# A two-layer gated graph convolution with a routed feed-forward block: order of work on ScalarE, GpSimd, VectorE and TensorE, and the gate product in 8 steps for 12

## The reference

```python
def layer(x, row, col, edge_type, w, gate_w, root, bias):        # w: 2 x 512 x 512, from 30 basis matrices
    x_j = x[col]
    msg = [sigmoid(x_j @ gate_w[r]) [:, None] * x_j @ w[r] for r in (0, 1)]
    agg = segment_sum(where(edge_type == 0, msg[0], msg[1]), row)
    return agg + x @ root + bias
h = relu(layer(layernorm(x), ...))
x = x + layer(h, ...)
t = layernorm(x)
shared = two experts, gelu(t @ w1 + b1) @ w2 + b2, each 512 -> 64 -> 512
probs = softmax(t @ gate_w.T + gate_b)            # 8 experts
routed = sum over the two largest probs of prob * expert(t)
x = x + shared + routed
```

## Time and profile before

| | |
|---|---|
| median of 3 runs (lowest to highest) | 1832.68 us (1831.2 to 1836.52) |
| the profiled execution, its time and its span | 1830.14 us, 1828.4 us |
| TensorE matmul busy | 1614.8 us (88%) |
| VectorE busy | 911.4 us (50%) |
| ScalarE busy | 724.4 us (40%) |
| GpSimd busy | 545.7 us (30%) |
| DMA | 270.45 MB, mean 148 GB/s |

### The profile page before, as it was taken

The page is one execution under the profiler, slowest core; times in us unless marked ns, Lnnn a source line. Parts: engine busy times, 40 slices in busy tenths (PEclk is TensorE's granted clock), DMA queues, the critical chain, the costliest instruction groups (busy, mean ns, idle before and its releaser), DMA issues. The chain is left out here.

```text
span 1828.4 us, 24688 instructions
## 1 busy us (share of the span) xinstructions
PE 1614.8 (88%) x7982; PEld 1271.0 (70%) x7982; DVE 911.4 (50%) x2116; ACT 724.4 (40%) x1168; POOL 545.7 (30%) x624
## 2 busy tenths in 40 slices
PE   3887788978888799999999924999999999999999
PEld 3554555757666577777888713887887888788887
DVE  4443444786664233333765525554655555455443
ACT  2333233445554122222565513434443444444342
POOL 3563111258885100000267633211221131122100
PEclk9999899989999799999999967999999999999999
DMA  8788978536665799998477661112211311221201
GB/s 252 219 235 153 269 232 232 186 117 140 112 117 83 216 280 277 279 277 261 155 163 132 115 161 69 69 70 92 115 70 74 134 69 69 102 105 69 79 26 41
DMA packets 72313, 270.45 MB, mean 148 GB/s; under 512 B 12532, under 2 KB 12532, under 8 KB 57122
## 3 DMA queue, kind: packets, MB, share of 16 engines
q1 hardware_dynamic: 51714, 223.82, 39.3%
q0 software_dynamic: 20512, 45.57, 13.7%
HBM read 179.82 MB, written 89.48 MB: 147 GB/s over the span
## 5 line engine op out<-in xcount | busy, mean ns | idle before, releaser
L796 POOL TENSOR_TENSOR zr<-zr,xr 128x2048 f32<-128x2048 f32 (+1 forms) x20 | 93.2, 4664 | 428.6 <-DMA xr<-in_x 428.6
L823 ACT ACTIVATE th<-bank 128x512 fp32r<-128x512 f32 x158 | 94.5, 598 | 231.2 <-PE bank L1039 210.0
L1019 PE MATMUL bank<-tth,w1h 128*128 128x512 f32 (+1 forms) x400 | 164.0, 410 | 0.0
L1280 DVE SCALAR_TENSOR_TENSOR tl<-bank,th 128x512 fp32r<-128x512 f32 x79 | 54.6, 692 | 209.7 <-ACT th L823 209.7
L1019 PE MATMUL bank<-ttl,w1h 128*128 128x512 f32 (+1 forms) x400 | 156.9, 392 | 0.0
L1019 PE MATMUL bank<-tth,w1l 128*128 128x512 f32 (+1 forms) x400 | 156.1, 390 | 0.0
L1019 PE MATMUL bank<-w2h,gtl 128*128 128x512 f32 x395 | 154.8, 392 | 0.0
L1019 PE MATMUL bank<-w2h,gth 128*128 128x512 f32 x395 | 154.7, 392 | 0.0
L1019 PE MATMUL bank<-w2l,gth 128*128 128x512 f32 x395 | 154.4, 391 | 0.0
L1019 PE MATMUL bank<-root1h,th 128*128 128x512 f32 x316 | 134.4, 425 | 16.3 <-DVE yout L1298 15.7
L723 POOL DMA_INDIRECT gx<-y,dst_slot x42 | 47.0, 1120 | 307.1 <-ACT xn_e L841 292.4
(11 more groups left out here) (200 smaller groups left out, 3904.5 us busy)
## 6 DMA issues: line engine op xcount, KB each, us to landing
basis_t<-in_gnn_basis SPq DMA_DIRECT2D x64, 896.0 KB
xin<-in_x SPq DMA_DIRECT2D x39, 512.0 KB, 6.0
y<-yout SPq DMA_DIRECT2D x39, 512.0 KB
xin<-y SPq DMA_DIRECT2D x39, 512.0 KB, 5.6
z<-yout SPq DMA_DIRECT2D x39, 512.0 KB
zr<-z SPq DMA_DIRECT2D x19, 1024.0 KB, 4.8
xr<-in_x SPq DMA_DIRECT2D x19, 1024.0 KB, 6.8
out<-zr SPq DMA_DIRECT2D x19, 1024.0 KB, 3.9
```

Source lines behind the costliest of these rows:

```text
L796: pool.tensor_tensor(zq, zq, xr[:, q.mod(2), 0:n, :], ALU.add).then_inc(s_zx, 1)
L823: act.activation(th_a[:, s, :], tpb[s][:], f).then_inc(s_hi, 1)
L1019: ins = pe.matmul(out_ap, a(k), b(k), start=first, stop=last)
L1280: ins = dve.scalar_tensor_tensor(out=tl_a[:, s, :], in0=tpb[s][:], scalar=0.0, in1=th_a[:, s, :].bitcast(F32), op0=ALU.max, op1=ALU.subtract)
```

## The change

1. ScalarE, part A: `norm` of the tile two ahead stands before `w_evac` in `step`.
2. Part B: the edge rows' rstd is shared out. VectorE makes the variance plus EPS right behind the statistics (`edge_stats`), GpSimd only the power (`edge_root`), VectorE the shift (`edge_shift`) one pair step later, ahead of the turned low parts. The statistics stand last in the pair step, behind `edge_lo` and `edge_gate`.
3. Parts B and D: `gx` has six buffers for four. A gather waits for the normalisation of an edge tile two earlier than before, three pairs are gathered ahead, and in GpSimd's `ahead` the gather stands before the power.
4. `xr` moves to the place of `root2h`, free when C is done. SyncE loads x of groups 0 and 1 right behind the expert weights, at the start of D, and z of both after the last scatter. VectorE adds x of group 0; GpSimd adds group 1 behind the rstd of group 0, and group 2 once the routing weights of group 0 are known.
5. TensorE: the gate weights' high and low parts lie side by side in one stationary tile `gwp`, so the gate product takes 8 products for 12 (high and low of the tokens against both; low x low comes in as well). `route_a` first adds the two parts (one `tensor_reduce`), and the chain has 14 steps for 13.
6. TensorE, group 0: the up blocks 0 and 1 stand before and behind the turning of the logits by token, ahead of the transposed routing weights.

```diff
 # placement
         top[0] = late
+        xr = sb("xr", [P, 2, QT, H])
+        assert top[0] <= root2_end
         zr = sb("zr", [P, 4, QT, H])
-        xr = sb("xr", [P, 2, QT, H])
-        gx = sb("gx", [P, 4, H])
+        gx = sb("gx", [P, 6, H])
-        gwh = sb("gwh", [P, KC, P], F32R)
-        gwl = sb("gwl", [P, KC, P], F32R)
+        gwp = sb("gwp", [P, KC, P], F32R)
+        lgs = sb("lgs", [P, QT, NE])
 # SyncE
+            for q in range(2):
+                load_x(Pos(q))
             scattered(sp, 1)
-            for q in range(3):
-                load_group(Pos(q))
+            for q in range(2):
+                load_z(Pos(q))
+            load_group(Pos(2))
 # GpSimd
-                    wait(pool, s_xn, e - 3)
-                    pool.indirect_dma_start(out=gx[:, e % 4, :], ...
+                    wait(pool, s_xn, e - 5)
+                    pool.indirect_dma_start(out=gx[:, e % 6, :], ...
-            def edge_rstd(pr):
-                s = slice(pr.two, pr.two + 2)
-                pool.wait_ge(s_eag, pr.e + 2)
-                rstd_of(erstd[:, s, 0], enmr[:, s, 0], emv[:, s, 0], emv[:, s, 1], s_ers, Pos(pr.U), s_est)
+            def edge_root(pr):
+                r = erstd[:, pr.two:pr.two + 2, 0]
+                pool.wait_ge(s_ers, pr.U + 1)
+                pool.tensor_tensor(r, r, minus_half[:, 0:2], ALU.pow).then_inc(s_erp, 1)
             def ahead(phase, u):
                 a4, a5 = pair_at(phase, u + 4), pair_at(phase, u + 5)
+                if a5 and a5.u > 2:
+                    gather(a5)
                 if phase == SB and a4:
-                    edge_rstd(a4)
-                if a5 and a5.u > 1:
-                    gather(a5)
+                    edge_root(a4)
-            for q in range(3):
-                add_x(Pos(q))
-                if q < 2:
-                    group_rstd(Pos(q))
+            group_rstd(Pos(0))
+            add_x(Pos(1))
+            group_rstd(Pos(1))
+            pool.wait_ge(s_cw3, 1)
+            add_x(Pos(2))
 # ScalarE
                 if a1:
                     hi(a1)
+                if a2 and st.phase == SA:
+                    norm(a2)
                 c = w_step(st)
                 if c is not None:
                     w_evac(c)
-                if a2 and st.phase == SA:
-                    norm(a2)
 # TensorE
-                product(bank[7][:, 0:n], lambda k: gwh[:, k, :], lambda k: gwl[:, k, :],
-                        lambda k: tth[:, s, k, 0:n], lambda k: ttl[:, s, k, 0:n], range(KC)).then_inc(s_lg, 1)
+                for k in range(KC):
+                    for part, t in enumerate((tth, ttl)):
+                        ins = pe.matmul(bank[7][:, 0:n], gwp[:, k, :], t[:, s, k, 0:n],
+                                        start=k + part == 0, stop=k + part == KC)
+                ins.then_inc(s_lg, 1)
             logits(Pos(0))
+            up(Pos(0), 0)
             logits_by_token(Pos(0))
+            up(Pos(0), 1)
             transpose_weights(Pos(0))
 # VectorE
+                s = slice(pr.two, pr.two + 2)
+                dve.wait_ge(s_eag, pr.e + 2)
+                dve.tensor_scalar(erstd[:, s, 0], emv[:, s, 1], EPS, None, ALU.add).then_inc(s_ers, 1)
+            def edge_shift(pr):
+                s = slice(pr.two, pr.two + 2)
+                dve.wait_ge(s_erp, pr.U + 1)
+                dve.scalar_tensor_tensor(out=enmr[:, s, 0], in0=emv[:, s, 0], scalar=-1.0, in1=erstd[:, s, 0],
+                                         op0=ALU.mult, op1=ALU.mult).then_inc(s_est, 1)
                 if a2:
                     edge_same(a2)
+                if a3 and phase == SB:
+                    edge_shift(a3)
                 if a1:
                     edge_turned_lo(a1)
...
-                if a4 and phase == SB:
-                    edge_stats(a4)
                 if a2:
                     edge_lo(a2)
                 if a3:
                     edge_gate(a3)
+                if a4 and phase == SB:
+                    edge_stats(a4)
+                chain(dve.tensor_reduce(lgs[:, 0:n, :], parts, AX_X, ALU.add))
+            dve.wait_ge(s_xr[0], 16)
+            dve.wait_ge(s_zin[0], 16)
+            for j in range(QT):
+                ins = dve.tensor_tensor(zr[:, 0, j, :], zr[:, 0, j, :], xr[:, 0, j, :], ALU.add)
+            ins.then_inc(s_zx, 1)
             q_stats(Pos(0), range(QT), True)
```

More of the change, by code:

```diff
@@ L281, in gnn_moe_kernel @@
         s_ystore = [sem(f"y_stored{i}") for i in range(2)]
-        s_gx = [sem(f"gathered{i}") for i in range(4)]
+        s_gx = [sem(f"gathered{i}") for i in range(6)]
         s_est = sem("edge_stats_known")
@@ L302, in gnn_moe_kernel @@
         s_eag = sem("edge_mean_and_variance")
-        s_ers = sem("edge_rstd")
+        s_ers = sem("edge_variance_raised")
+        s_erp = sem("edge_rstd")
         s_dup = sem("repeats_counted")
@@ L588, in load_group, with load_z @@
                     return
+                load_z(q)
+                load_x(q)
+            def load_z(q):
                 n = q_tiles(q)
@@ L721, in gather @@
                 for e, t in ((pr.e, 2 * pr.u), (pr.e + 1, 2 * pr.u + 1)):
-                    wait(pool, s_xn, e - 3)
-                    pool.indirect_dma_start(out=gx[:, e % 4, :], out_offset=None, in_=x if pr.phase == SB else y1,
+                    wait(pool, s_xn, e - 5)
+                    pool.indirect_dma_start(out=gx[:, e % 6, :], out_offset=None, in_=x if pr.phase == SB else y1,
                                             in_offset=bass.IndirectOffsetOnAxis(ap=dst_slot[:, t:t + 1], axis=0))\
-                        .then_inc(s_gx[e % 4], 16)
+                        .then_inc(s_gx[e % 6], 16)
             def scatter(pr):
@@ L763, in _ @@
                 pair_rstd(Pos(g))
-            for u in range(2):
+            for u in range(3):
                 gather(Pair(SB, u))
@@ L836, in edge_xn @@
                         wait(act, s_est, pr.U + 1)
-                        act.activation(xn_e[:, s, :], gx[:, s, :], ACT.Identity, bias=enmr[:, s, :],
+                        act.activation(xn_e[:, s, :], gx[:, e % 6, :], ACT.Identity, bias=enmr[:, s, :],
                                        scale=erstd[:, s, :]).then_inc(s_xn, 1)
                     else:
-                        wait(act, s_gx[s], 16 * (e // 4 + 1))
-                        act.activation(xn_e[:, s, :], gx[:, s, :], ACT.Relu).then_inc(s_xn, 1)
+                        wait(act, s_gx[e % 6], 16 * (e // 6 + 1))
+                        act.activation(xn_e[:, s, :], gx[:, e % 6, :], ACT.Relu).then_inc(s_xn, 1)
             def edge_gated(pr):
@@ L1193, in group @@
                 for c in range(FC):
-                    up(q, c)
+                    if q.i is not None or q.k or c > 1:
+                        up(q, c)
                     if c:
@@ L1303, in edge_stats @@
                     s = e % 4
-                    wait(dve, s_gx[s], 16 * (e // 4 + 1))
+                    wait(dve, s_gx[e % 6], 16 * (e // 6 + 1))
                     wait(dve, s_xn, e - 3)
-                    dve.bn_stats(ebn[:, s, :], gx[:, s, :]).then_inc(s_ebn, 1)
+                    dve.bn_stats(ebn[:, s, :], gx[:, e % 6, :]).then_inc(s_ebn, 1)
                 for e in (pr.e, pr.e + 1):
@@ L1498, in route_a @@
                 wait(dve, s_lgx, q.times(1, 1))
-                chain(dve.tensor_tensor(lg[:, 0:n, :], bank[7][:, 0:n * P].rearrange("p (j e) -> p j e", e=P)[:, :, 0:NE],
+                parts = bank[7][:, 0:n * P].rearrange("p (j k e) -> p j e k", k=P // NE, e=NE)[:, :, :, 0:2]
+                chain(dve.tensor_reduce(lgs[:, 0:n, :], parts, AX_X, ALU.add))
+                chain(dve.tensor_tensor(lg[:, 0:n, :], lgs[:, 0:n, :],
                                         gbias[:].rearrange("p (a e) -> p a e", a=1).to_broadcast([P, n, NE]), ALU.add))
```

12 lines of the change are left out of this document (7 added, 5 removed).

## The result

The changed kernel took 1764.32 us (median of 4 runs, 1759.02 to 1766.07) where before took 1833.78 in the same comparison: ratio 0.9616, interval 0.9589 to 0.9643, so some 70 us less. The profiled execution took 1765.87 us, its span 1764.1 against 1828.4. Forecast was 1761, range 1743 to 1786. The total lies 3 us from the forecast, but its terms don't fit as well: in this pair of traces A gave some 9 us less than forecast and the hand-over 6 less, and B, with its earlier start, 8 us more. (B's earlier start stands in the first line of the table, with A.)

The account below looks back on a forecast made before the run. TensorE leads in most parts, with time to be had in layer 1 nodes, the expert hand-over, and layer 1 edges, where GpSimd has no idle time. -42 - 12 + 2.5 - 13.6 - 6.4 = -71.5, from 1832.7 to 1761 us, range 1743 to 1786.

Parts of the forecast that it names:

- A, -42: Layer 1 nodes: normalising ahead of the w evacuation removes 32 TensorE waits of 1.45 us, less deductions: -42 us.
- For both I allow 1.5 us: Layer 1 nodes: 1.5 us taken off the gain for GpSimd's scarce idle time while writing records and for fuller DMA queues.
- 2.9 for the standstill: Layer 1 nodes: TensorE's 10.63 us standstill behind the slow transfer of row numbers grows by 2.9 us.
- B, -12: Layer 1 edges: scatter period falls from 9.10 to 8.15 us over 15 pairs, 14.3 us, less 2 charged at the start.
- D, +2.5: Layer 2 edges: two 1 MB x loads at the start delay the scatter chain, +2.5 us, bounds 0 and +7.5.
- Hand-over, -13.6: Hand-over to the experts: -11.7 us up to the transposed routing weights, the rest behind them; -13.6, bounds -9 and -17.
- Experts, -6.4: Expert groups: four fewer logit products save 0.92 us in each of seven written-out groups, nothing in the loop: -6.4 us.
- 1: Rival: layer 1 nodes are held by the DMA queues and half the gain is lost, 1782 us; chance 0.12.
- 2: Rival: layer 1 edges keep their period, VectorE and GpSimd waiting for each other in turn, 1775 us; chance 0.14.
- 3: Rival: in layer 1 edges that mutual wait closes over the scatters too, 14.4 us per pair, 1886 us; chance 0.03.
- 4: Rival: the twelve expert groups of the loop gain too, 11 us, giving 1750 us; chance 0.12.
- 5: Rival: in expert groups GpSimd's add beats VectorE's third difference; in 15 groups 67 us lost, 1828 us; chance 0.03.

Follow-up runs that it names:

- norm_alone: The kernel before with only the normalisation of part A moved ahead of the evacuation of w rows: ratio 0.9818 to before, 33 us less.
- edges_alone: The kernel before with only the edge part (six gather buffers, gathers three pairs ahead, only the power on GpSimd): ratio 0.9913 to before, 16 us less.
- logits_alone: The kernel before with only the gate product in 8 steps for 12: ratio 0.9967 to before, 6 us less.
- best_x_later: Changed kernel with row numbers turned on VectorE, x addition in four, and x loads after layer 2 edges' tenth scatter pair: 0.9463 to before; 0.9458 with loads at start.
- add_in_four: The changed kernel with GpSimd's addition of x to z as four instructions for one: ratio 0.9554 to before, against 0.9645 for the changed kernel.
- before_again: The kernel before once more, no edit, for a second trace: 68.5 us from z's issue to the first down block, span 1837.0 us.
- cw_unguarded: The changed kernel without GpSimd's wait for group 0's routing weights ahead of group 2's addition: ratio 0.9662 to before, against 0.9645 for the changed kernel.
- rows_after: The changed kernel with row numbers turned on VectorE and written in rows of 64 bytes: ratio 0.9524 to before, against 0.9645 for the changed kernel.

## Why the prediction came out right, point by point

The mechanisms held in the main, but that the total came within 3 us is in part luck. In the traced pair three terms are off by 6 to 9 us and in part cancel (A and the hand-over gave less, B more), and the spans differ by 64.3 us where the medians differ by 69.5; the ratio of 0.9645 gives 65.

- **A, -42: the mechanism right, one deduction too small.** The 32 waits are gone, 46.4 us. "For both I allow 1.5 us" is the term that was mis-sized. I set GpSimd's 1.55 us of idle per pair against the shrunken period and found them equal, but the last record transfer waits 5 to 7 us at its issue whatever the kernel (5.5 in the trace of before, 6.82 after), and with no idle left that lands on TensorE: 6.3 us here, 5.2 to 5.9 in the other fast traces. The other deduction, 2.9 for the standstill, measured 7.3 in this pair of traces, but by the means of all traces 2.9 (13.1 against 10.2): right, and the 7.3 is the pair's. For this pair 46.4 - 6.3 - 7.3 = 32.8, with 3.7 of B's earlier start 36.5; read: 36.8. By the means it would be about 38. norm_alone measured -33 by its ratio, 30 to 36 with its interval, so my own sign, "I am wrong if A gains less than 35 us", came up by the ratio and not by the traces.
- **B, -12: period right, one charge wrong.** 15 x 0.95 = 14.3 was exact. The first gap, 11.77 us, fell to 9.49 as well: B 16.4 us shorter in all. The 2 us charged for VectorE's wait at the end of A didn't come; B started 3.7 us earlier instead (edges_alone against logits_alone, 0.9 of it already there when TensorE reaches tile 64 of A). I had this in the bound of -20 and not in the value. My sign for it, no idle time of VectorE at the shift, was wrong: it waits 27.0 us there in 19 pairs, 1.4 each, and that costs nothing, since 8.15 is set by the scatters.
- **D, +2.5: right in kind.** Third pair 21.8 to 22.4 us behind the first in the six traces with x loads at the start, 19.4 to 21.2 in the seven without any: 2.1 us later in the mean. All of D takes 166.3 us against 165.4 in the mean, 1.0 more, with ranges that overlap (164.2 to 169.1, 163.0 to 168.8), so the cost over all of D isn't told from scatter. The row of 10.5 us, and in best_x_later the one of 13.4, shows the two streams slowing each other, as by the Trainium skill, DMA: Bandwidth & Descriptors, Issuing engines are not separate DMA queues; its consequence of 7.5 us, if none of it is hidden, isn't borne out.
- **Hand-over, -13.6: right up to the weights, wrong behind them.** Six traces with the old code have the weights 45.9 to 48.6 us behind z, mean 47.5, against 36.8: -10.7 (forecast -11.7). The first trace of before was the fastest of the six. Its 12 logit products ended 1.6 to 2.7 us earlier than in the others, at a mean granted clock of 0.77 over the 85 us from z, where the others have 0.71 to 0.75. Behind the weights I forecast -5.6 + 2.7 + 1 = -1.9; it is 22.1 us for 21.2, +0.9. The "+1" for the adds beside VectorE's differences is the failed term: the first difference alone lost 3.3 us, and add_in_four gets 5.3 back there. In all, from z's issue to the first down block, 8.0 us are gained on the first trace of before and 9.8 on the mean of the six, for -13.6.
- **Experts, -6.4: right.** The three written-out groups between the first and fourth store take 102.7 and 101.9 us for 104.6 in norm_alone: 0.6 to 0.9 per group. The loop gains nothing, and TensorE waits 14.6 / 11 = 1.3 us at the fourth down block (forecast 1.1), where before_again has 3.8 in 9. The first traced pair holds a gift of 4 us in group 3, of which scatter in the loop took back 2.5.
- **Rivals.** 1 (A held back by half its gain) came half true, by two stalls and not by queues that hold every period: the middle of A is full at a share of 0.92. The total missed it since B gave more. 2 and 3 fell with the period of 8.15, 4 with logits_alone. 5 didn't happen as a whole, but its mechanism is what shapes the hand-over and the loop's period. By the Trainium skill, SBUF — State Buffer, Who interferes with whom, VectorE instructions with two inputs in the state buffer contend with GpSimd's reads; the trace agrees for the differences (both inputs there), while the output addition, with one input from a bank, stays at 0.68 to 0.69 us in every group. A copy with one input there was held as well (4.53 us in cw_unguarded), which that sentence doesn't cover.

What stays open: why the standstill differs from one execution to the next, where the 8 us lie by which the gain of rows_after exceeds what its trace shows, and why the gains of rows_after and add_in_four didn't add up fully. Items 4 and 6 of the change were never run without each other; from z's issue to the end the changed kernel's traces gain 14.7 us in the mean and logits_alone 6.3, which leaves some 8 for the two together.

## What to carry to other kernels

When an edit makes a stage run at its engine's full rate, look through the whole stage for the one-off stalls that its idle time used to swallow; here two of them took 14 us of 46 in one pair of traces, and 8 to 9 in the mean of all. An instruction moved behind the thing that it disturbed will disturb what comes next: either cut it into pieces as long as the wait that one can bear, or follow its new neighbours as well. And take a row that carries a term from two traces of the kernel where there are two: single rows here were off by 2 to 7 us.

## What the runs showed of the hardware

- One transfer of 5376 single 2-byte words (10.5 KB) took 28.0 us (before) and 32.1 (after), and loads of x issued meanwhile 24 to 28 us in place of 7.2. Turning the words on VectorE (0.23 us) and writing rows of 64 bytes, later in A, brought each write down to 6.1 to 6.5 us with no standstill.
- A VectorE difference with both inputs in the core's memory, or a copy there, that starts during a GpSimd add is held until the add's end: 2.26, 3.99, 4.53 and 5.14 us for 0.69 or 0.2. With GpSimd's add in four pieces of 1.44 us (5.9 in all, for 4.8) it takes 1.44 in the loop, and at most 1.84 elsewhere.
- Two loads of 1 MB at D's start delayed the third pair of scatters by 2.1 us, and the same loads at its tenth pair delayed the next by 5.3, where the bytes at C's 279 GB/s would take 7.5.
